# A gated cross-attention and feed-forward block on one core: other engines for the first normalisation, another order of bo, rstd and the last sums, and three first loads moved to ScalarE's queue

## The reference

```python
def _layernorm(x, axis=-1, eps=1e-05):
    m = jnp.mean(x, axis=axis, keepdims=True)
    v = jnp.var(x, axis=axis, keepdims=True)
    return (x - m) / jnp.sqrt(v + eps)
...
        Q = (query @ Wq.T + bq).reshape(n, len_q, N_HEADS, HEAD_DIM).transpose(0, 2, 1, 3)
        K = (input_flatten @ Wk.T + bk).reshape(n, len_in, N_HEADS, HEAD_DIM).transpose(0, 2, 1, 3)
        scores = jnp.einsum('nhqd,nhkd->nhqk', Q, K)
        scores = jnp.where(input_padding_mask[:, None, None, :], -jnp.inf, scores)
        attn = jax.nn.softmax(scores, axis=-1)
        V = jnp.broadcast_to(input_flatten[:, None], (n, N_HEADS, len_in, D_MODEL))
        out = jnp.einsum('nhql,nhld->nhqd', attn, V)
        return out @ Wo.T + bo
...
        w = (weights >= 0.0).astype(x.dtype) * 2.0 - 1.0
        y = jnp.einsum('bsi,oi->bso', x, w)
        y = y * scale + bias
        y = jnp.clip(y, -MAX_VAL, MAX_VAL)
...
    x = x + jnp.tanh(g_xattn[0]) * _L0_xattn_ref(_layernorm(x, axis=-1), ctx_1024, mask_BxS2_bk0, ...)
    x = x + jnp.tanh(g_ffn[0]) * _L0_ffn_ref(_layernorm(x, axis=-1), L0_ffn_weights, L0_ffn_scale, L0_ffn_bias)
```

## Time and profile before

| | |
|---|---|
| median of the runs | 77.05 us (76.86 to 77.10, 3 runs) |
| the profiled execution | 77.18 us |
| its span, first to last instruction | 75.4 us |
| TensorE (PE) busy | 68.4 us, 91% of the span |
| GpSimd (POOL) busy | 55.4 us, 73% |
| VectorE (DVE) busy | 56.2 us, 75% |
| ScalarE (ACT) busy | 43.3 us, 57% |
| chain that ended last | PE 58%, POOL 19%, DVE 7%, DMA 7% |

### The profile page before, as it was taken

How to read it: one execution, slowest core, us unless ns; L and a number is a source line. 1 busy time by engine, 2 the same in 40 slices (tenths; PEclk the granted TensorE clock), 3 DMA queues, 4 the chain that set the end, 5 groups by cost and what they waited for, 6 DMA issues and landing times.

```text
span 75.4 us, 1597 instructions
## 1 busy us (share of the span) xinstructions
PE 68.4 (91%) x509; PEld 64.1 (85%) x509; DVE 56.2 (75%) x182; ACT 43.3 (57%) x118; POOL 55.4 (73%) x113
## 2 busy tenths in 40 slices
PE   4999969999999999999999999999999998998600
PEld 4997858999999999999999999999999988865400
DVE  0071956993874868998898989899959897578870
ACT  1503326579979639963976495669549607554100
POOL 4000488889889985998699889989952999999700
PEclk9999999999999999999999999999999999999995
DMA  0987999999940000004002100400040004004044
GB/s 3 277 274 250 308 253 297 252 366 358 328 159 20 4 0 4 9 4 135 0 0 78 61 0 9 138 1 0 0 139 0 0 9 139 0 4 139 0 139 139
DMA packets 8228, 8.10 MB, mean 107 GB/s; under 512 B 536, under 2 KB 8092, under 8 KB 8220
## 3 DMA queue, kind: packets, MB, share of 16 engines
q1 hardware_dynamic: 8212, 8.00, 34.1%
q10 hardware_dynamic: 8, 0.00, 0.0%
HBM read 5.90 MB, written 2.10 MB: 106 GB/s over the span
## 4 chain that ended last, share of the span: by engine, by line
PE 58%; POOL 19%; DVE 7%; DMA 7%; issue 3%; SPq 2%; ACT 1%; DVEq 1%; POOLq 0%
PE ps_K L621 11%; PE ps_Z L621 11%; PE ps_xT L616 8%; PE ps_S L621 8%; PE ps_F L621 7%; PE ps_O L696 7%; DMA x_sb<-in_x_dram 7%; POOL xb_sb L373 4%; POOL y_biased L377 4%; PE ps_cT L616 3%; POOL y_clip L350 3%; POOL rstd L325 2%; POOL out_sb L356 2%; PE ps_S L688 2%; POOL xn L318 1%
## 5 line engine op out<-in xcount | busy, mean ns | idle before, releaser
L373 POOL TENSOR_TENSOR xb_sb<-x_sb,bo_g 128x256 f32<-128x256 f32 x16 | 12.8, 821 | 0.1
L377 POOL TENSOR_TENSOR y_biased<-y_scaled,bias_g 128x256 f32<-128x256 f32 x14 | 10.5, 773 | 0.2
L222 ACT ACTIVATE p_sb<-t_sb,smin 128x128 f32<-128x128 f32 x16 | 6.4, 401 | 7.1 <-DVE smin L454 7.1
L621 PE MATMUL ps_Z<-woT_hi,cT_hi 128*128 128x256 f32 x32 | 9.7, 303 | 0.0
L212 ACT ACTIVATE K_sb<-ps_K,u_col 128x256 f32<-128x256 f32 x14 | 5.9, 474 | 6.5 <-PE ps_K L621 6.5
L465 DVE SCALAR_TENSOR_TENSOR x_sb<-ps_O,recip_p,xb_sb 128x256 f32<-128x256 f32 x14 | 6.1, 479 | 4.0 <-PE ps_O L696 4.0
L621 PE MATMUL ps_Z<-woT_hi,cT_lo 128*128 128x256 f32 x32 | 9.0, 283 | 0.0
L621 PE MATMUL ps_K<-cT_hi,wqk_hi 128*128 128x256 f32 x30 | 8.8, 294 | 0.3 <-DVE wqk_lo L546 0.3
L621 PE MATMUL ps_Z<-woT_lo,cT_hi 128*128 128x256 f32 x32 | 9.0, 282 | 0.0
L621 PEld LDWEIGHTS ps_S<-K_sb,xT 128*128 128x128 f32 x64 | 8.1, 191 | 0.8 <-issue 0.4
L621 PE MATMUL ps_S<-K_sb,xT 128*128 128x128 f32 x64 | 8.6, 277 | 0.2 <-ACT K_sb L248 0.2
(11 more groups left out here) (128 smaller groups left out, 204.3 us busy)
## 6 DMA issues: line engine op xcount, KB each, us to landing
ctx_sb<-in_ctx_dram SPq DMA_DIRECT2D x8, 256.0 KB, 7.6
x_sb<-in_x_dram SPq DMA_DIRECT2D x8, 256.0 KB, 7.6
out_dram<-out_sb SPq DMA_DIRECT2D x7, 256.0 KB, 2.1
wq_sb<-in_L_xattn_Wq_dram SPq DMA_DIRECT2D x1, 256.0 KB, 2.9
wk_sb<-in_L_xattn_Wk_dram SPq DMA_DIRECT2D x1, 256.0 KB, 3.2
wo_sb<-in_L_xattn_Wo_dram SPq DMA_DIRECT2D x1, 256.0 KB, 5.2
mask_u<-in_mask_BxS_bk_dram SPq DMA_DIRECT2D x1, 256.0 KB, 5.7
w_sb<-in_L_ffn_weights_dram SPq DMA_DIRECT2D x1, 256.0 KB, 6.9
```

Source lines behind the costliest of these rows:

```text
L222: nc.scalar.activation(p_sb[:, g % 2, b], t_sb[:, g % 2, b], ACT.Exp, scale=-1.0, bias=smin[:, r:r + 1], accum_out=psum_p[:, r:r + 1]).the ...
L373: nc.gpsimd.tensor_tensor(xb_sb[:, r], x_sb[:, r], bo_g[:], ALU.add).then_inc(xb_done, 1)
L377: nc.gpsimd.tensor_tensor(y_biased[:, g % 2, b], y_scaled[:, g % 2, b], bias_g[:, 0], ALU.add).then_inc(biased_done, 1)
L621: last = nc.tensor.matmul(dst, lhsT, rhs, start=(n == 0), stop=(n == len(pairs) - 1))
```

## The change

The start: Wk, bq, bk and x(0), in this order, are issued from ScalarE's queue, and SyncE's queue begins with Wq, ctx(0), Wo. VectorE takes the first low part of the folded weights ahead of the statistics of x(0), adds eps for group 0, and normalises x(0) itself as (x - mean) * rstd once GpSimd has taken the power; the 1 that GpSimd's bias term held is added when VectorE evicts the transposed x(0). GpSimd expands the first mask ahead of the norm of x(1). TensorE transposes x(0) ahead of the gates.

The rounds: from i = 2 on GpSimd adds bo of group i ahead of the rstd of x1(i - 1), and in round 6 it adds bo of group 7 there too. Round 6 of VectorE leaves out the final sum of group 4, so that the residual of group 6 follows the scaling of y at once; the sum follows the split of x1(6).

The end: GpSimd clips y(5) ahead of rstd of x1(6). The eps for the last variances is added by VectorE for both batches at once, and not by ScalarE. TensorE does both halves of the feed-forward of group 6 ahead of the two transposes of the last softmax weights. The sum of the first half of group 7 stands ahead of the clip of the second.

The diff, without the declarations of buffers and semaphores:

```diff
@@ -153,9 +153,7 @@
                 sp.dma_start(ctx_sb[:, rows(g), :], ctx_rows[:, rows(g), :]).then_inc(ctx_loaded[g], 16)
 
             sp.dma_start(wq_sb[:], wq.rearrange("(c p) d -> p c d", p=P)).then_inc(wq_loaded, 16)
-            sp.dma_start(wk_sb[:], wk.rearrange("(c p) d -> p c d", p=P)).then_inc(wk_loaded, 16)
             load_ctx(0)
-            load_x(0)
             sp.dma_start(wo_sb[:], wo.rearrange("(c p) d -> p c d", p=P)).then_inc(wo_loaded, 16)
             sp.dma_start(mask_u8[:], mask.rearrange("(o b) k -> o b k", o=1).to_broadcast([P, B, P])
                          ).then_inc(mask_loaded, 16)
@@ -187,8 +185,10 @@
 
         @block.scalar
         def _(act):
+            act.dma_start(wk_sb[:], wk.rearrange("(c p) d -> p c d", p=P)).then_inc(wk_loaded, 16)
             for k, v in enumerate((bq, bk)):
                 act.dma_start(vec_rows[k * DC:(k + 1) * DC, :], v.rearrange("(c p) -> c p", p=P)).then_inc(vecs_loaded, 16)
+            act.dma_start(x_sb[:, rows(0), :], x_rows[:, rows(0), :]).then_inc(x_loaded[0], 16)
 
             def evict_cT_hi(g):
                 act.wait_ge(cT_prod, g + 1)
@@ -196,7 +196,7 @@
 
             def normalise_x(g):
 
-                act.wait_ge(nmr_x_done, g + 1)
+                act.wait_ge(nmr_x_done, g)
                 for b in range(GB):
                     r = g * GB + b
                     nc.scalar.activation(xn[:, r], x_sb[:, r], ACT.Identity, scale=rstd_x[:, r:r + 1],
@@ -283,36 +283,30 @@
                 act.wait_ge(x1T_prod, L + b + 1)
                 nc.scalar.copy(xT[:, 0, :, b * P:(b + 1) * P], last_x1T[b]).then_inc(x1T_hi_done, 1)
 
-            for b in range(GB):
-                r = L * GB + b
-                act.wait_ge(mv_1_done, r + 1)
-                nc.scalar.activation(ve_1[:, r:r + 1], mv_1[:, r, 1:2], ACT.Identity, bias=eps_col[:, 0:1]
-                                     ).then_inc(ve_last_done, 1)
-
         @block.gpsimd
         def _(pool):
             nc.gpsimd.memset(ident[:], 0.0).then_inc(zeroed, 1)
             nc.gpsimd.memset(minus_half[:], -0.5).then_inc(half_ready, 1)
             nc.gpsimd.memset(ones_row[:], 1.0).then_inc(ones_ready, 1)
-            nc.gpsimd.memset(eps_col[:], EPS).then_inc(eps_ready, 1)
             pool.wait_ge(zeroed, 1)
             nc.gpsimd.affine_select(out=ident[:], in_=ident[:], compare_op=ALU.not_equal, fill=1.0, base=0,
                                     pattern=[[-1, P]], channel_multiplier=1).then_inc(ident_ready, 1)
 
             def norm_of_x(g):
+
                 pool.wait_ge(mv_x_done, GB * (g + 1))
                 nc.gpsimd.tensor_scalar(ve_x[:, rows(g)], mv_x[:, rows(g), 1], EPS, None, ALU.add).then_inc(ve_x_done, 1)
-                pool.wait_ge(ve_x_done, g + 1)
+                pool.wait_ge(ve_x_done, g)
                 nc.gpsimd.tensor_tensor(rstd_x[:, rows(g)], ve_x[:, rows(g)], minus_half[:], ALU.pow).then_inc(rstd_x_done, 1)
-                pool.wait_ge(rstd_x_done, g + 1)
+                pool.wait_ge(rstd_x_done, g)
                 nc.gpsimd.tensor_tensor(mr_x[:, rows(g)], mv_x[:, rows(g), 0], rstd_x[:, rows(g)], ALU.mult).then_inc(mr_x_done, 1)
-                pool.wait_ge(mr_x_done, g + 1)
+                pool.wait_ge(mr_x_done, g)
                 nc.gpsimd.tensor_scalar(nmr_x[:, rows(g)], mr_x[:, rows(g)], -1.0, 1.0, ALU.mult, ALU.add
                                         ).then_inc(nmr_x_done, 1)
 
             def normalise_x(g):
 
-                pool.wait_ge(nmr_x_done, g + 1)
+                pool.wait_ge(nmr_x_done, g)
                 for b in range(GB):
                     r = g * GB + b
                     nc.gpsimd.tensor_scalar(xn[:, r], x_sb[:, r], rstd_x[:, r:r + 1], nmr_x[:, r:r + 1],
@@ -326,7 +320,7 @@
 
             def rstd_of_last_x1(b):
                 r = L * GB + b
-                pool.wait_ge(ve_last_done, b + 1)
+                pool.wait_ge(ve_last_done, 1)
                 nc.gpsimd.tensor_tensor(rstd_1[:, r:r + 1], ve_1[:, r:r + 1], minus_half[:, 0:1], ALU.pow
                                         ).then_inc(rstd_1_done, 1)
 
@@ -382,11 +376,11 @@
                     add_bias_of(g, b)
 
             pool.wait_ge(half_ready, 1)
-            norm_of_x(0)
-            normalise_x(0)
-            norm_of_x(1)
+            pool.wait_ge(ve_first_done, 1)
+            nc.gpsimd.tensor_tensor(rstd_x[:, rows(0)], ve_x[:, rows(0)], minus_half[:], ALU.pow).then_inc(rstd_first_done, 1)
             pool.wait_ge(mask_loaded, 16)
             mask_terms(0)
+            norm_of_x(1)
             normalise_x(1)
             pool.wait_ge(tanh_ready, 1)
             pool.wait_ge(bo_loaded, 16)
@@ -402,16 +396,21 @@
                     add_bias(i - 2)
                     if i + 2 < G:
                         norm_of_x(i + 2)
-                rstd_of_x1(i - 1)
-                add_bo(i)
+                if i == 1:
+                    rstd_of_x1(0)
+                    add_bo(1)
+                else:
+                    add_bo(i)
+                    if i == L - 1:
+                        add_bo(L)
+                    rstd_of_x1(i - 1)
                 mask_terms(i + 1)
                 if i in (3, 4):
                     scale_weights(i - 3)
-            add_bo(L)
             add_bias(L - 2)
-            rstd_of_x1(L - 1)
             pool.wait_ge(lim_ready, 2)
             clip(L - 2)
+            rstd_of_x1(L - 1)
             add_x1(L - 2)
             add_bias(L - 1)
             clip(L - 1)
@@ -537,19 +536,26 @@
             for c in range(DC):
                 nc.vector.tensor_scalar(wq_neg[:, c], wq_sb[:, c], -1.0, wq_off[:, c:c + 1], ALU.mult, ALU.add
                                         ).then_inc(wq_neg_ready, 1)
-            stats_x(0)
             dve.wait_ge(wqk_hi_ready, 1)
             nc.vector.tensor_tensor(wqk_lo[:, 0], ps_wqk[0], wqk_hi[:, 0].bitcast(F32), ALU.subtract
                                     ).then_inc(wqk_lo_ready, 1)
+            stats_x(0)
+            dve.wait_ge(mv_x_done, GB)
+            nc.vector.tensor_scalar(ve_x[:, rows(0)], mv_x[:, rows(0), 1], EPS, None, ALU.add).then_inc(ve_first_done, 1)
             split_cT(0)
             dve.wait_ge(wqk_hi_ready, DC)
             nc.vector.tensor_tensor(wqk_lo[:, 1], ps_wqk[1], wqk_hi[:, 1].bitcast(F32), ALU.subtract
                                     ).then_inc(wqk_lo_ready, 1)
             dve.wait_ge(ps_u_ready, 1)
             nc.vector.tensor_copy(u_col[:], ps_u).then_inc(u_ready, 1)
+
+            dve.wait_ge(rstd_first_done, 1)
+            for b in range(GB):
+                nc.vector.tensor_scalar(xn[:, b], x_sb[:, b], mv_x[:, b, 0:1], rstd_x[:, b:b + 1], ALU.subtract, ALU.mult
+                                        ).then_inc(xn_first_done, 1)
             stats_x(1)
             dve.wait_ge(xT_prod, 1)
-            nc.vector.tensor_copy(xT[:, 0], ps_xT).then_inc(xT_done, 1)
+            nc.vector.tensor_scalar(xT[:, 0], ps_xT, 1.0, None, ALU.add).then_inc(xT_done, 1)
             dve.wait_ge(woT_hi_ready, 1)
             nc.vector.scalar_tensor_tensor(out=woT_lo[:], in0=by_chunk(z_bank), scalar=tanh_g[:, 0:1],
                                            in1=woT_hi[:].bitcast(F32), op0=ALU.mult, op1=ALU.subtract
@@ -573,13 +579,14 @@
                 if i >= 2:
                     clip_y(i - 2)
                 scale_y(i - 1)
-                if i >= 2:
+                if 2 <= i < L - 1:
                     add_x1(i - 2)
                 if i + 3 < G:
                     stats_x(i + 3)
             residual(L - 1)
             stats_x1(L - 1)
             split_x1T(L - 1)
+            add_x1(L - 3)
             mask_and_min(L)
             dve.wait_ge(rstd_1_done, L)
             for b in range(GB):
@@ -598,14 +605,16 @@
                 stats_last_x1(b)
             for b in range(GB):
                 aggregate_last_x1(b)
+            dve.wait_ge(mv_1_done, GB * G)
+            nc.vector.tensor_scalar(ve_1[:, rows(L)], mv_1[:, rows(L), 1], EPS, None, ALU.add).then_inc(ve_last_done, 1)
             dve.wait_ge(pool_clip_done, 2 * GB)
             nc.vector.tensor_tensor(out_sb[:, rows(L - 1)], y_clip[:, (L - 1) % 2], x1_sb[:, rows(L - 1)], ALU.add
                                     ).then_inc(out_done, 1)
             last_y(0)
             clip_last(0)
             last_y(1)
+            add_last_x1(0)
             clip_last(1)
-            add_last_x1(0)
             add_last_x1(1)
 
         @block.tensor
@@ -622,7 +631,10 @@
                 return last
 
             def transpose_x(g):
-                pe.wait_ge(xn_done, GB * (g + 1))
+                if g == 0:
+                    pe.wait_ge(xn_first_done, GB)
+                else:
+                    pe.wait_ge(xn_done, GB * g)
                 if g >= 3:
                     pe.wait_ge(x1T_lo_done, g - 2)
                 elif g >= 1:
@@ -682,8 +694,8 @@
```

(13 more changed lines are left out.)

## The result

The changed kernel takes 79.31 us (median, 78.62 to 79.82, 4 runs) against 76.95 for the kernel before (76.81 to 77.10, 4 runs): a ratio of 1.026 with a 95% interval of 1.0216 to 1.0303. Forecast were 76.53 and a range of 75.9 to 77.1. The profile shows the slowest of the four executions, 79.82 us with a span of 78.0; its differences to the profiled execution of before are therefore about 0.3 us larger than those of the medians.

The account below looks back on a forecast made before the run. TensorE, busy from 13.30 to 55.40 us, bounds the middle, so only start and end could move: +0.18 + 0 - 0.70 = -0.52, from the median of 77.05 to 76.53 us, range 75.9 to 77.1.

Parts of the forecast that it names:

- Wq's lateness: Start, loads: Wq lands later with Wk in flight beside it, taken as +0.55 us, at most +0.74.
- rival C: Start: bq and bk late behind Wk's packets; a loss if they land after 4.97, 77.7 us at 5.6; chance 0.10.
- M: Start of the first Wk by Wq product on TensorE, at 5.53 us in the kernel before.
- three signs of being wrong: First scores moved over 0.6 us; TensorE not busy throughout the middle; last minimum waiting for the moved addition.
- first leg: Start, M to K(0)'s first weight load: 4.07 us becomes 4.04, a gain of 0.03, none really.
- second leg: Start, K(0)'s first weight load at 9.60 to the first scores: 3.69 us becomes 3.35, a gain of 0.34.
- S: Start of the first scores on TensorE, at 13.29 us in the kernel before; forecast at about 13.45.
- The middle: From first scores to 55.40 us TensorE is busy throughout; bo ahead of rstd costs 0, at most +0.2.
- three terms: End: TensorE's gap ahead of x1(6) closed (-0.41), last attention product nearer (-0.10), last rstd earlier (-0.19); together -0.70 us.
- rival B: No change, 77.0: Wq +0.74; at the end only TensorE's gap counts, moved addition or busy GpSimd delaying; chance 0.18.
- The second term: End: last two TensorE feeds unbroken by a transpose, shortening VectorE's wait of 0.16 at 68.22: -0.10 us (0 to -0.16).
- The last rstd: End: it no longer starts right behind GpSimd's clip, only the variance counts: -0.19 us (0 to -0.30).

Follow-up runs that it names:

- e1: The kernel before with only the three loads (Wk, x(0) to ScalarE's queue, Wk ahead of bq and bk) moved: 79.35 us, ratio 1.0294.
- e5: The kernel before with the two tiny gate loads ahead of bq and bk in ScalarE's queue: 78.37 us, one run, no ratio.
- e9: The kernel before with four warm-up products instead of six ahead of the vectors and four instead of three behind, so TensorE pauses: 78.00 us, ratio 1.0116.
- e4: The changed kernel with ten instead of six warm-up products ahead of the vectors' transpose: 78.23 us, ratio 1.0128 against the kernel before.
- e3: The changed kernel with bq and bk issued ahead of Wk in ScalarE's queue: 79.47 us, scattered, no ratio.
- e2: The changed kernel with all engine orders kept but the loads issued as in the kernel before: 76.77 us, ratio 0.9988 against the kernel before.
- e6: e2 with x(0) alone moved to ScalarE's queue, behind bq and bk: 77.29 us, ratio 1.0041 against the kernel before.
- e7: e2 with the final sum of group 4 ahead of the split of x1(6): 76.83 us, ratio 0.9968 against the kernel before.
- e8: e7 with the last eps added batch by batch, each right behind its variance: 76.24 us, ratio 0.9916 against the kernel before.

## Why the prediction was wrong

**The loads: the step that failed.** I had Wq's lateness as the price of the loads (+0.55) and put the bias vectors aside, because Wk's bytes "landed at 4.41". That time belonged to the other layout, in which Wk stood behind Wq in SyncE's queue. With the two in flight together Wk landed at 0.72 + 4.2 = 4.92, and the vectors behind it at 1.86 + 3.69 = 5.55. They were turned at 5.69, beyond the 4.97 that I had given as the point from which the change turns into a loss, so rival C, at 0.10, was what happened. e1 shows that the loads carry it, and e5 splits the delay. Wq landed 0.94 later (4.61 against 3.67), more than the upper bound of 0.74, but what sets M is the vectors. Even with the vectors on time the forecast would have missed: with +0.94 for Wq in place of 0.55, and 0.23 at the end in place of 0.70, the sum is about 77.4 (an estimate: 76.53 + 0.39 + 0.47), beyond the range. Two of my three signs of being wrong came, the moved first scores and the last minimum behind the moved sum.

**What I had not in the sum at all.** By rival C's own formula the vectors at 5.69 cost 5.69 - 4.97 = 0.72, that is 77.8; the time was 79.3. The leg from M to the first weight load of K(0), 4.07 before, became 12.82 - 7.30 = 5.52. That is 1.45 more, because the two Wk by Wq products took 1.91 each instead of 1.07 and 1.03, and the transposes of the context between them 1.06 instead of 0.66; that these are 2.12 together and the leg grew by less is because TensorE's weight loads had also waited in it, 0.46 at its end. e9 and e5, pauses with both weights loaded as before, show that TensorE's standing still ahead of the vectors is enough to bring this about, without other traffic of large loads; e5 has all the matmuls of zeros of the kernel before. e4 and e3 show which pauses do it: where TensorE had become faster in its matmuls of zeros before it stopped at 4.91 or 5.41, a pause of 0.77 or 1.51 left the products short; where it was still slow when it stopped, at 3.97 or 3.11, one of 0.47 or 0.64 left them slow. In the kernels without a pause ahead of the vectors (before, e2, e6, e7, e8) the second product took 1.03 each time, in those with one in the slow stretch (the changed kernel, e1, e5, e9) 1.37 to 1.91. The Trainium skill, "TensorE: Matmul & The Clock Gate", section "Part 1: The HAM clock gate (the "warmup" mystery)", says that TensorE's array is throttled by default and that activity releases it, between 1.2 and 2.4 GHz; the durations agree (1.91 to 1.07 is near two to one, and so are e4's first and last matmuls of zeros), while the clock column reads 1.00 in that stretch, so that the clock as the cause is argued from durations and not seen.

In the profile the start then adds up: M +1.77 (the vectors 1.79), the first leg +1.45, the second leg 16.12 - 12.82 = 3.30 against 3.69, -0.39: +2.83, where I had +0.18.

**The orders at the start: right, and in part by luck.** e2 has S 0.38 earlier; I had 0.37. Its second leg is 3.37 (9.54 to 12.91), I had 3.35; but the terms as I listed them make 3.30 with the overlap of 0.05 that I named, and the four transposes stood for 0.58 until the gates (10.39 to 10.97), not 0.44, while other pieces were shorter. The first leg was 4.08 and gave nothing (I had 0.03), and 0.07 of the 0.38 came from M, 5.46 against 5.53, which the orders don't touch. In the changed kernel this gain is not seen apart from the loads: e1, with the old orders, has a second leg of 3.25, as short as in e5 and e9; I take it that with slow products the work beside TensorE catches up, which no run shows by itself.

**The middle: right.** TensorE is busy for 42.09 of 42.10 us from e2's first scores on, and for all of 42.10 in the changed kernel from 16.13 on, as in the earlier trace rows.

**The end: a second step that failed.** I had -0.70, in three terms, all of them ahead of the first y of the last group. Counted from S this y comes 0.03 earlier in the changed kernel and 0.02 in e2 (70.24 - 12.91 = 57.33): the three terms together brought almost nothing. The other 0.20 of the 0.23 lie behind it, where the change puts the sum of the first half ahead of the clip of the second, so that the first half is sent out earlier; my sum has no term for this, and no run tried it alone, so that this cause is argued. The gap of 0.41 ahead of x1(6) was closed, but the sum that I moved "in time that VectorE spends waiting for the last scores" stood behind the split, not in that wait, and it took 1.12 us beside GpSimd's sums of group 5 (1.88 for two; in e7, where VectorE's sum is over by then, 1.44). So the last minimum came when the sum was done, which is half of rival B: what I put at nothing was the cost of the moved sum. e7 puts the sum into the wait and has 0.39 of it back. The second term, the wait at 68.22, was right in kind: the first of the last residuals stands where it did from S (70.41 - 16.12 = 54.29), but the second follows it without a wait and comes 0.21 earlier (70.84 - 16.12 against 68.22 - 13.29), where I had 0.10.

The last rstd (-0.19) starts 0.29 earlier measured from S in e2 (69.28 - 12.91 = 56.37, against 69.95 - 13.29 = 56.66); most of this is the second residual's, so the term's own part is less than 0.1. And all of it was given back: with one eps for both batches VectorE's sum of group 6 starts at 69.11, just ahead of the power, which then takes 1.45 for two where it took 1.19, and the first y waits for it at 70.24. In e8 the power is first, and 0.30 comes back; its first y stands at 69.96 - 13.40 = 56.56 from S, 0.79 ahead of the kernel before, which is what my three terms were to give (0.70). The Trainium skill, "SBUF — State Buffer", section "🔬 SBUF: two separate sides", says that a VectorE operation with two SBUF inputs and a GpSimd operation that reads SBUF hold one shared pair of ports by turns, whichever starts first, for the whole instruction; both places agree with it in direction (0.76 to 1.12; 1.19 to 1.45, and 1.21 when the power starts first). It does not show the other way round: VectorE's sum of group 6, started 0.11 behind the power in e8 and 0.08 behind it in the kernel before, took 0.68 and 0.69, as long as when it came first. e7 and e8 changed order and not the ports, so that the lock is argued and the order is shown.

**What stays open.** e2's profile is 0.6 us shorter than that of before, its runs only 0.1% (up to 0.5% within the interval). A part is which execution was profiled: e2's took 76.63, below its median, that of before 77.18, above its own. The first product alone took between 1.07 and 1.77 us in kernels whose TensorE didn't pause (before, e2, e6, e7, e8), which moves S by some tenths from one execution to the next; whether that is the whole of the difference was not tried.

## What to carry to other kernels

A small load that the first step needs goes ahead of large ones in its queue: here 1 KB behind 256 KB came 1.25 us later, and a landing time read from one layout of queues says nothing of another. That alone did not rescue this change: with the vectors first (e3) it was Wk that came late. Where TensorE is kept busy with products of zeros until the first data arrive, price a late arrival twice: by the delay, and by the slow products behind a pause that comes before TensorE has become faster (e9: about 1 us in all for a pause of 0.64), or lengthen the warm-up (e4). A step moved into another engine's slack is to be placed in the wait itself and looked at together with what the other engine runs at that moment: e7 and e8, two moves of order, turned orders that measured as nothing into 0.8%.

## What the runs showed of the hardware

In the changed kernel two queues did not fill faster than one: in the first 3 us 49 GB/s against 84, and both weights landed after 3.9 and 4.2 us where they had taken 2.9 and 3.2. In e3, with the vectors first and Wk issued 0.87 behind Wq, the first 3 us moved 97 GB/s, and it was Wk that came 5.3 us after its issue while Wq lost nothing (3.57). The rule that the prediction took from "DMA: Bandwidth & Descriptors" (the Trainium skill), that loads of several engines share the DMA engines, agrees with the changed kernel, where both weights are later; in e3 the sharing was not even.

In these runs the length of TensorE's first products went by whether it had become faster before it paused, and not by how long the pause was: 1.91 after pauses of 0.47 to 1.72 that began by 3.97 in slow matmuls of zeros (e5, e9, e1, the changed kernel), 1.10 and 1.13 after pauses of 0.77 and 1.51 that began at 4.91 and 5.41 behind faster ones (e4, e3). In the changed kernel's slow stretch the clock column read 1.00.
